# Register reads, sort keys and setup order in a graph kernel: one edit of three parts

## The reference

```python
msg = x[src] + edge_attr
agg = jax.ops.segment_sum(msg, dst, num_segments=N)
h = jax.nn.relu(agg @ W1 + b1) @ W2 + b2
h = (h - mean(h)) * rsqrt(var(h) + EPS) * ln_w + ln_b      # over all of h
sub = h - gn_ms * mean(h, axis=0)
h = gelu(sub * rsqrt(mean(sub ** 2, axis=0) + EPS) * gn_w + gn_b)
out = layernorm(x + (h + x), axis=-1)
```

## Time and profile before

| | us |
|---|---|
| median of 3 runs | 811.84 (811.63 to 813.36) |
| profiled execution | 805.35 |
| its span | 803.0 |
| mean granted TensorE clock | 0.963 of full |

### The profile page before, as it was taken

How to read it: one execution, slowest core, us unless ns; L and a number is a source line. 1 busy time by engine, 2 the same in 40 slices (tenths; PEclk the granted TensorE clock), 3 DMA queues, 4 the chain that set the end, 5 groups by cost and what they waited for, 6 DMA issues and landing times.

```text
span 803.0 us, 25641 instructions
## 1 busy us (share of the span) xinstructions
PE 688.2 (86%) x9447; PEld 620.2 (77%) x9447; DVE 667.6 (83%) x1186; ACT 396.5 (49%) x858; POOL 78.6 (10%) x68
## 2 busy tenths in 40 slices
PE   3685799998999989999899898998989989999850
PEld 3573788888888878888789887898878888788730
DVE  6765988899898988989889898898988889825585
ACT  3723365346653466434664346633565335614464
POOL 2222010101101011010101101011010110000000
PEclk9987799999999999999999999999999999999965
DMA  6858246356463563635636366363662646331005
GB/s 158 293 165 285 90 148 204 105 163 206 128 200 121 167 206 112 212 109 184 206 93 213 110 201 206 84 203 125 204 205 81 196 134 206 102 107 61 0 0 159
DMA packets 88856, 123.47 MB, mean 154 GB/s; under 512 B 8479, under 2 KB 84348, under 8 KB 88635
## 3 DMA queue, kind: packets, MB, share of 16 engines
q1 hardware_dynamic: 82220, 116.30, 45.8%
q0 software_dynamic: 5616, 5.25, 2.3%
q10 hardware_dynamic: 1000, 1.65, 0.9%
HBM read 119.10 MB, written 4.03 MB: 153 GB/s over the span
## 4 chain that ended last, share of the span: by engine, by line
PE 37%; DVE 26%; issue 18%; DVEq 7%; DMA 5%; ACT 5%; ACTq 1%; SPq 0%; POOLq 0%
PE bank L735 20%; DVE pool_m L1020 20%; PE bank L710 5%; PE bank L661 4%; DVEq L947 4%; PE bank L792 3%; PE bank L782 3%; ACT counts L553 2%; DVE onehot L931 2%; DMA pool_m<-in_x_dram 2%; DMA agg<-in_src_dram 1%; PE bank L633 1%; DMA begins<-listed,tile_slot 1%; DMA edges<-in_edge_attr_dram 1%; ACT x_hi L522 1%
## 5 line engine op out<-in xcount | busy, mean ns | idle before, releaser
L553 ACT CAST counts<-bank 128x490 fp32r<-128x490 f32 x625 | 314.2, 668 | 312.9 <-PE bank L710 311.4
L735 PE MATMUL bank<-counts,x_hi 128*128 128x250 f32 x1225 | 290.6, 282 | 25.5 <-ACT counts L553 25.5
L735 PE MATMUL bank<-counts,x_lo 128*128 128x250 f32 x1225 | 287.0, 279 | 0.0
L735 PEld LDWEIGHTS bank<-counts,x_hi 128*128 128x128 f32 x1225 | 231.3, 189 | 29.3 <-ACT counts L553 29.3
L1020 DVE TENSOR_TENSOR pool_m<-value_row,turned_lo 128x3328 bf16<-128x3328 bf16 x125 | 235.8, 1887 | 0.2
L735 PEld LDWEIGHTS bank<-counts,x_lo 128*128 128x128 f32 x1225 | 232.1, 190 | 0.0
L710 PE MATMUL bank<-pool_m 128*128 128x98 bf16 x3125 | 200.3, 210 | 23.1 <-DVE pool_m L1020 20.4
L710 PEld LDWEIGHTS bank<-pool_m 128*128 128x128 bf16 x3125 | 161.4, 99 | 62.1 <-ACT counts L553 43.7
L1020 DVE TENSOR_TENSOR pool_m<-value_row,turned_key 128x2548 bf16<-128x2548 bf16 x125 | 184.5, 1476 | 0.0
L661 PE MATMUL bank<-edges,onehot 128*32 128x128 f32 x3228 | 122.1, 286 | 5.2 <-DMA edges<-in_edge_attr_dram 5.2
L661 PEld LDWEIGHTS bank<-edges,onehot 128*32 128x32 f32 x3228 | 85.1, 113 | 17.9 <-DVE onehot L931 4.2
(11 more groups left out here) (151 smaller groups left out, 405.3 us busy)
## 6 DMA issues: line engine op xcount, KB each, us to landing
edges<-in_edge_attr_dram SPq DMA_DIRECT2D x134, 768.0 KB, 5.2
out_dram<-pool_m SPq DMA_DIRECT2D x6, 512.0 KB
agg<-in_dst_dram SPq DMA_DIRECT2D x1, 768.0 KB
agg<-in_src_dram ACTq DMA_DIRECT2D x1, 768.0 KB
listed<-agg ACTq DMA_DIRECT2D x1, 768.0 KB
begins<-listed,tile_slot POOLq DMA_INDIRECT x27, 7.4
begins<-listed,row_slot POOLq DMA_INDIRECT x27, 5.5
w<-in_L_gnn_W_dram SPq DMA_DIRECT2D x2, 128.0 KB, 2.8
```

The source lines that it names most:

```text
L553: nc.scalar.copy(counts[:, :, k * nodes:(k + 1) * nodes].rearrange("p q (i m) -> p q i m", m=PAIR), cps[k % RING][:, 0:nodes * NT].rearran ...
L735: last = nc.tensor.matmul(sps[:, 0:CHUNK], part[:, q, :], counts[:, q, :], start=(q == 0 and part is x_hi), stop=(q == NT - 1 and part is ...
```

## The change

It has three parts.

1. **Registers.** In `even` and `odd` the base nodes are no longer read together at the start. Each is read just ahead of its `add`, which mostly follows a `mark_batch`; one (`base3`) is read behind batch 4.
2. **Keys and counts.** The key was `hi * 2 + node + 98 * node * (node - 1)`, whose last term moves invalid nodes out of the range of keys. It becomes `node * 49 + hi`, where invalid nodes fall out of the range by themselves: one instruction less in the chain (`STEPS` 9 instead of 10). The columns of a bank are then ordered node, source instead of pair, source, node. So ScalarE's copy reads them for each source with a step of 49 words over the ten nodes, instead of in neighbouring twos.
3. **Setup.** ScalarE's queue issues the `src` loads first and the loads of the tiles' last words behind them. VectorE packs the list first, and only then computes the bounds and makes search 0. The signs get a buffer for each set (`below`, 14 of them, in the room of `counts` behind `pair_row`) and a semaphore of their own; ScalarE makes all 14 in a row, without waiting for TensorE, and copies `x` behind them instead of between piece 1 and piece 2.

```diff
+        below = nc.alloc_sbuf_tensor_at("below", [P, (len(PIECES) - 1) * SETS, SEARCH * PAIRS], BF16,
+                                        offset=counts_at + (NPAIR + 7) // 16 * 32 + 32)
...
-        below = behind[:, 0:BELOW * SEARCH * PAIRS].rearrange("p (s v) -> p s v", s=BELOW)
...
+            act.dma_start(src_rows[0:EVEN, :], src_full[0:EVEN, :]).then_inc(src_loaded, 16)
+            act.dma_start(src_rows[EVEN:FULL, :], src_full[EVEN:FULL, :]).then_inc(src_loaded, 16)
+            act.dma_start(src_rows[FULL:GROUPS, 0:REST], src_rest).then_inc(src_loaded, 16)
             act.wait_ge(rows_padded, 1)
...
-            act.dma_start(src_rows[0:EVEN, :], src_full[0:EVEN, :]).then_inc(src_loaded, 16)
-            act.dma_start(src_rows[EVEN:FULL, :], src_full[EVEN:FULL, :]).then_inc(src_loaded, 16)
-            act.dma_start(src_rows[FULL:GROUPS, 0:REST], src_rest).then_inc(src_loaded, 16)
...
-                for i in sets:
-                    n = piece * SETS + i
-                    act.wait_ge(below_used, max(SETS, n + 1 - BELOW))
-                    nc.scalar.activation(below[:, n % BELOW, 0:(b - a) * PAIRS], pair_row[:, a * PAIRS:b * PAIRS],
-                                         ACT.Sign, bias=tile_bias[:, i:i + 1]).then_inc(below_ready, 1)
-
-            search(1, range(EARLY))
+                for i in range(SETS):
+                    nc.scalar.activation(below[:, (piece - 1) * SETS + i, 0:(b - a) * PAIRS], pair_row[:, a * PAIRS:b * PAIRS],
+                                         ACT.Sign, bias=tile_bias[:, i:i + 1]).then_inc(signs_ready, 1)
+
             act.wait_ge(listed_ready, 1)
...
-            search(1, range(EARLY, SETS))
+            search(1)
+            search(2)
             act.wait_ge(x_loaded, 32)
...
-            search(2, range(SETS))
...
-                    nc.scalar.copy(counts[:, :, k * nodes:(k + 1) * nodes].rearrange("p q (i m) -> p q i m", m=PAIR),
-                                   cps[k % RING][:, 0:nodes * NT].rearrange("p (i q m) -> p q i m", q=NT, m=PAIR)
+                    nc.scalar.copy(counts[:, :, k * nodes:(k + 1) * nodes],
+                                   cps[k % RING][:, 0:nodes * NT].rearrange("p (n q) -> p q n", q=NT)
                                    ).then_inc(banks_free, 1)
...
-            search(0)
-            dve.wait_ge(below_used, SETS)
-            read_tiles(*PIECES[0])
-            dve.engine_nop().then_inc(tiles_read, 1)
-            stage_tile(0)
-
             dve.wait_ge(dst_loaded, 48)
             dve.wait_ge(src_loaded, 48)
...
             dve.engine_nop().then_inc(listed_ready, 1)
+            dve.wait_ge(ends_loaded, 32)
+            link(dve.tensor_scalar(tile_end[:, :], tile_end_i[:, :], 1.0 / PAIR, None, ALU.mult), setup, steps)
+            link(dve.tensor_scalar(tile_bias[:, :], tile_end[:, :], -1.0, -0.25, ALU.mult, ALU.add), setup, steps)
+            dve.engine_nop().then_inc(ends_ready, 1)
+            search(0)
+            dve.wait_ge(below_used, SETS)
+            read_tiles(*PIECES[0])
+            dve.engine_nop().then_inc(tiles_read, 1)
+            stage_tile(0)
...
-                prep_chain(dve.scalar_tensor_tensor(node_f[0:PAIRS, :], hi_i[0:PAIRS, :], float(PAIR), node_f[0:PAIRS, :],
+                prep_chain(dve.scalar_tensor_tensor(node_f[0:PAIRS, :], node_f[0:PAIRS, :], float(NT), hi_i[0:PAIRS, :],
                                                     ALU.mult, ALU.add), n + 7)
-                prep_chain(dve.scalar_tensor_tensor(node_f[0:PAIRS, :], junk[0:PAIRS, 0:P], float(KEYS), node_f[0:PAIRS, :],
-                                                    ALU.mult, ALU.add), n + 8)
...
-                base0, base1 = base_of(first), base_of(first + 1)
...
-                add(first, 0, base0, c + 1)
+                add(first, 0, base_of(first), c + 1)
...
-                base2, base3, base4 = base_of(first + 2), base_of(first + 3), base_of(first + 4)
...
                 mark_batch(c, 3)
-                add(first + 2, 0, base2, c + 1)
+                add(first + 2, 0, base_of(first + 2), c + 1)
                 mark_batch(c, 4)
+                base3 = base_of(first + 3)
                 put(first + 4, 0)
```

More of the change, by code:

```diff
@@ L69 @@
 PIECES = ((0, 4), (4, 14), (14, 25))
-EARLY = 4
-BELOW = 3
 SEARCH = 11
@@ L254, in gnn_kernel @@
         below_ready = sem("below_ready")
+        signs_ready = sem("signs_ready")
         below_used = sem("below_used")
@@ L498, in _, with search @@
                           ).then_inc(listed_stored, 16)
-            def search(piece, sets):
+            def search(piece):
                 a, b = PIECES[piece]
@@ L629, in search @@
                     n = piece * SETS + i
-                    pe.wait_ge(below_ready, n + 1)
+                    if piece == 0:
+                        pe.wait_ge(below_ready, i + 1)
+                    else:
+                        pe.wait_ge(signs_ready, n + 1 - SETS)
                     for c in range(a, b):
-                        of = first_below[:, i] if piece == 0 else below[:, n % BELOW]
+                        of = first_below[:, i] if piece == 0 else below[:, n - SETS]
                         last = nc.tensor.matmul(tile_ps[0:PAIRS, c:c + 1], of[:, (c - a) * PAIRS:(c - a + 1) * PAIRS],
@@ L856, in _ @@
                               ).then_inc(consts_ready, 1)
[L857 to L860, removed]
             def search(piece):
@@ L970, in prep_chain @@
                 dve.wait_ge(prep, count)
-            STEPS = 10
+            STEPS = 9
             def stage_row(c):
@@ L1081, in even @@
                     mark_batch(c + 1, 1)
-                    add(first + 1, 1, base1, c + 1)
+                    add(first + 1, 1, base_of(first + 1), c + 1)
                     mark_pair(p, 7)
@@ L1104, in odd @@
                 mark_batch(c + 1, 1)
-                add(first + 4, 0, base4, c + 1)
+                add(first + 4, 0, base_of(first + 4), c + 1)
                 mark_pair(p + 1, 1)
```

## The result

| timed side by side | before | after |
|---|---|---|
| median | 812.25 (811.63 to 813.36, 4 runs) | 806.14 (805.41 to 806.67, 4 runs) |
| ratio | | 0.9924 [0.9912, 0.9936] |
| profiled execution, span | 805.35, 803.0 | 806.58, 804.3 |
| mean granted TensorE clock | 0.963 | 0.961 |

The change saves 6.1 us of 812.25. The forecast was 791.4 with a range from 783 to 802: the sign was right, the size was not, and the time lies outside the range. One row of the table is odd. By the two profiles alone the change gains nothing, and by the times it gains 6 us. That gap is half of this study.

What follows compares the result with a forecast made beforehand. Prediction: TensorE bounds the product, ScalarE the count while fed, starved by VectorE's late tables. Odd chunks 5.0, even 10.8, chunk 0 1.6, setup 3.0: 20.4 us off 811.84 gives 791.4; range 783 to 802.

Steps and rivals of the forecast that it cites:

- the sum's last: Final step: 20.4 us of gain taken from the profiled 805.35, and likewise from the timed median 811.84, giving 791.4.
- 5.0 + 10.8 + 1.6 = 17.4 us: Register reads moved: 12 odd chunks at 0.42 us, 12 even ones at 0.9, and chunk 0's two reads, 1.6.
- the copies' end: End of the odd count: ScalarE's last eleven copies, fed in time, take 5.29 us instead of 5.72.
- Reads hidden: VectorE's register reads, some 0.70 us each, cost nothing behind a table or pair of tables.
- Rival 1: Register reads not hidden behind VectorE's tables: loop gains 8.4 us, with setup 3 makes 800 us; chance 0.11.
- The new wait for batch 3: VectorE's batch 3 waits about 1 us for TensorE's fifth bank in odd chunks, but VectorE has it to spare.
- Rival 2: Batch 3's wait for the fifth bank plus hand-overs loses half the loop's 15.8 us: 799 us; chance 0.08.
- Keys at nothing: VectorE's key chain, one instruction shorter in 26 chains, saves 8 us of its time, hidden by the product: counted 0.
- Counts read node by node at nothing: ScalarE's copies of counts from PSUM with a step of 49 words keep the contiguous pace: 0 us.
- rival 3: ScalarE's count copies slower with words apart; at twice the time an element, 1,085 us; chance 0.06.
- Setup 3.0: Before the loop: earlier packing and signs let edge sums start sooner, 3.0 us gained, bounds 0 and 5.
- Rival 4: The setup gives nothing, the loop gains as forecast: 794 us; chance 0.07.

Runs made afterwards that it cites:

- 812 kind: Comparisons in which the unchanged kernel before took 812.0 to 813.3 us; seen on the same chip as the other kind.
- keys: Kernel before with only the shorter key and the counts read node by node: 812.59 us, ratio 1.0004 to before.
- setup: Kernel before with only the reordered setup: 809.69 us, ratio 0.9971 to before.
- 805 kind: Comparisons in which the unchanged kernel before took 805.2 to 805.7 us; seen on the same chip as the other kind.
- before again: Kernel before, unchanged, profiled once more: 805.16 us (one run).
- after again: The changed kernel, unchanged, run once more beside before at 805.21 us: 790.69 us, ratio 0.9820.
- six banks: The changed kernel with GpSimd's near gather held until six banks of the count are done: 790.32 us (0.9720, 812 kind), 789.58 us (0.9804, 805 kind).
- keys again: Kernel before with only the shorter key and the counts read node by node, second run, before at 813.29 us: 813.55 us, ratio 1.0002.
- registers again: Kernel before with only the register reads moved behind the tables, second run, before at 805.21 us: 793.70 us, ratio 0.9851.
- setup again: Kernel before with only the reordered setup, second run, before at 813.29 us: 811.57 us, ratio 0.9983.

## Why the prediction was wrong

**The step that failed is the sum's last.** It read "The profiled execution took 805.35 (span 803.0), so 784.9; the median of the runs shown is 811.84, which less the same amount gives 791.4". That takes the profile for a picture of the timed runs, off by a constant. It was a picture of the other kind. The kernel before was never profiled in the 812 kind; but keys and setup, which have its registers, show there a stall in nearly every count that the profile lacks, and the stall covers most of what the registers cost. The prediction gave the registers 5.0 + 10.8 + 1.6 = 17.4 us; alone they brought 2.4 in the 812 kind (811.96 to 809.59) and 11.5 in the 805 kind.

- In the 805 kind a pair goes from 50.66 to 49.73 us, and the loop from the first to the last product from 607.1 (before again, 91.64 to 698.74) to 596.6 (after again, 87.59 to 684.21).
- In the 812 kind it goes from 51.2 or 51.3 (keys, setup) to 51.18. The late tables were hidden behind the late third copy.

What the stall is, as far as shown: GpSimd's near gather runs at the front of the count, and in the 812 kind ScalarE takes up the third bank only near the end of that instruction, 0.6 us late in odd chunks (13.94 against 13.32) and 0.8 in even ones (14.38 against 13.56); SyncE is 0.9 us late in odd ones (14.01 against 13.15), VectorE 0.3 (14.07 against 13.78). That it hangs on the gather is shown by moving it. That it makes the whole difference of the kinds for after is shown by six banks: 790.3 and 789.6. That signals are what is late is read from three engines that start together, and was not tried alone. Nor is it simply that every signal waits until the gather ends. Behind product 16 of after (at 496.53) the gather comes 1 us later, and VectorE takes up the fifth bank in time, 0.25 us into it:

```profile
510.06 1.22 POOL L456 DMA_INDIRECT begins<-listed,row_slot  x1 [13.12 <-issue]
510.31 1.89 DVE L1016 TENSOR_TENSOR pool_m<-value_row,turned_lo 128x3328 bf16<-128x3328 bf16 x1 [0.87 <-PE bank L710]
```

In keys again SyncE starts a load 0.35 us late at 335.40 (13.73 behind its product, 13.38 in after again), 0.48 us before its gather ends (334.67 to 335.88), while ScalarE's third copy comes 0.18 us behind that end. Which signals are held, and why only some comparisons have it, stays open.

**The second fault is a size: the copies' end.** The prediction let ScalarE's last eleven copies take 10 x 0.47 + 0.59 = 5.29 us. They take 5.50 or 5.51. The last is 0.76 long in odd chunks and 0.81 or 0.82 in even ones, instead of 0.59 (311.15 less 310.39, 336.11 less 335.30 in after again): a copy's length grows in a row without idle time, from 0.58 to 0.85, while their pitch stays 0.46. And in odd chunks one pitch, ahead of the third last, is 0.58: that copy starts at 22.99 behind the product, 0.04 us after TensorE finished its bank, so ScalarE still loses 0.12 us there; ahead of that bank stands a half of the edge sums, and no table is late. Nine pitches of 0.46, that 0.58 and 0.76 make the 5.50. The product waits for the last end. So 0.42 a chunk in odd chunks became 24.95 - 24.74 = 0.21, and 0.9 in even ones became 25.68 - 24.98 = 0.7. The last even count was not late before (24.95 us from product to product in before again, 24.97 in after again) and gained nothing, which the prediction had not looked at. Twelve odd and eleven even ones are 2.5 + 7.7 = 10.2 us instead of 15.8, and the loop gained 607.1 - 596.6 = 10.5. Chunk 0 gave 1.0 to 1.4 (first product at 90.60 in registers again, 91.64 and 92.03 in the profiles of before) instead of 1.6. With 3.0 for the setup that sums to 14.4; the times say 14.5.

**Point by point.**

- *Reads hidden:* right. The idle ahead of `place` went from 34.1 to 3.0 us. VectorE now idles where it is early: in after again 11.0 us for TensorE's fifth banks and 14.0 for ScalarE's turned keys. The reads are seen beside tables: this one starts at 302.8 and its last register work at 303.4, and the `add` follows the table without a gap (two rows of VectorE's timeline and, between them, the read from the view by line):

```profile
302.06 1.48 DVE L1016 TENSOR_TENSOR pool_m<-value_row,turned_key 128x2548 bf16<-128x2548 bf16 x1
L945 DVEq TENSOR_LOAD <-base_i x1: 303/303/303, 302.8 to 302.8; - x1
303.45 0.28 DVE L953 TENSOR_TENSOR agg<-agg,bank 128x128 f32 x1
```

Rival 1 falls: in the 805 kind the loop gained the tables' lateness, less the copies' ends.

- *The new wait for batch 3:* right in place and nearly in size: 0.87 us in after again, 1.17 under the stall, forecast 1. It moved nothing: TensorE's wait for tables is absent from the profiles of after. Rival 2 falls.
- *Keys at nothing:* right, ratios 1.0004 [0.9994, 1.0014] and 1.0002 [0.9990, 1.0013], though this kernel also has the new counts and ran in the 812 kind alone, where a small gain could be covered.
- *Counts read node by node at nothing:* right. Ten copies take 4.89 us against 4.88. So rival 3 falls. The rule of the Trainium skill ("Advanced Engine Details and Errata", "PSUM Cachelines") that two consecutive fp32 values should lie together, which it states for matmuls, does not show in ScalarE's copies here: single words 49 apart go as fast as pairs.
- *Setup 3.0:* right in the sum, in part by luck. 3.0 us between after again and registers again (with the keys in it), 1.7 to 2.3 in the 812 kind. The edge sums start at 42.41 (forecast 42.6). On the way two terms missed in opposite senses: packing began at 13.74 and not 12.7, and the third comparison took 8.31 and not 9.32, since it no longer keeps step with the signs. The one was 1.0 worse than forecast, the other 1.0 better. Rival 4 falls.
- *Range:* the rivals all bent the gain inside one picture. None asked whether the picture was that of the timed runs, though 805.35 beside 811.63 to 813.36 stood in the table. A rival "the timed runs have a wait that the profile lacks, and it covers the registers" would have put the time at 812 less the setup and what is left: near 806 to 809 (an estimate made afterwards).

The best version over both kinds is after with the gather held to six banks: 790.3 against 813.3 (0.9720) and 789.6 against 805.2 (0.9804). It beats before in either kind, and after in the 812 kind (806.1, in another comparison); in the 805 kind it is 1.1 us below after, within what the intervals allow.

## What to carry to other kernels

When the profiled execution lies outside the timed runs, it may show another kernel's bottleneck: give a rival to that case, and price it at what the gain is if each wait you remove is already covered. Look at what GpSimd issues at the moment when the critical hand-over takes place; holding one gather back changed the time by 2% down in after (812 kind, across two comparisons) and by 2.7% up in before (805 kind). And a time saved at the end of a row of pipelined instructions counts from the end of the last, whose length is not that of the first.

## What the runs showed of the hardware

- While GpSimd ran an indirect gather of 125 rows (1.21 to 1.46 us), ScalarE, SyncE and VectorE started 0.3 to 0.9 us late behind TensorE in some comparisons (VectorE 0.3, ScalarE 0.6 to 0.8, SyncE 0.9), and with the same timing not at all in others. In one count (behind product 16) the gather started 1 us later, at 13.53 us behind the product, and that count had no stall, in after as in setup again (24.74 and 24.96 us from product to product, against 25.4 in the other odd counts).
- ScalarE's copies of 128x490 words keep a pitch of 0.46 us, but in a row without idle time one's length grows from 0.58 to 0.85 (after again, the 3rd to the 22nd copy of an odd count); behind a short wait it falls back (0.74), behind idle time to 0.58.
- A read of a register (0.30 us, some 0.70 with its register work) goes unseen behind a table of 1.5 to 1.9 us on the same engine.
